# Second mixture of a four-layer chain: the shared units first, routing beside the products, normalising inside the opening

## The reference

```python
x = x + jnp.tanh(g_ffn[1]) * _L1_ffn_ref(_layernorm(x, axis=-1), ...)

shared = jax.nn.silu(h @ sWg) * (h @ sWu) @ sWd          # 256 -> 2 x 128 -> 256
routing_weights = jax.nn.sigmoid(h @ gate_w.T)           # 16 experts
topk_w, topk_idx = jax.lax.top_k(routing_weights, 8)
topk_w = topk_w / (sum(topk_w) + 1e-06) * 2.5
comb = zeros((T, 16)).at[arange(T)[:, None], topk_idx].add(topk_w)
g, u = h @ Wg[e], h @ Wu[e]                              # for every e: 256 -> 128
eo = silu(g) * u @ Wd[e]                                 # 128 -> 256
result = shared + einsum('eth,te->th', eo, comb)
```

## Time and profile before

| | |
|---|---|
| median of 3 runs | 2523.2 us (2521.43 to 2532.25) |
| profiled execution | 2521.86 us, span 2520.1 us |
| mean granted clock of TensorE | 0.935 |
| busy over the span: PE, PEld | 2187.3 us (87%), 1830.6 us (73%) |
| DVE, ACT, POOL | 1848.3 us (73%), 1290.9 us (51%), 1241.4 us (49%) |
| second mixture: rstd ready to last addition | 1322.0 to 1679.95 us of the span |

### The profile page before, as it was taken

How to read it: one execution, slowest core, us unless ns; L and a number is a source line. 1 busy time by engine, 2 the same in 40 slices (tenths; PEclk the granted TensorE clock), 3 DMA queues, 4 the chain that set the end, 5 groups by cost and what they waited for, 6 DMA issues and landing times. The chain is left out here.

```text
span 2520.1 us, 44844 instructions
## 1 busy us (share of the span) xinstructions
PE 2187.3 (87%) x15434; PEld 1830.6 (73%) x15434; DVE 1848.3 (73%) x3715; ACT 1290.9 (51%) x3127; POOL 1241.4 (49%) x1693
## 2 busy tenths in 40 slices
PE   5969997599999889999976999978999993649996
PEld 2358886488888778888866888867888871327775
DVE  5856665699999899999974777764555547966775
ACT  2113332788888877888843333322444442436763
POOL 4903442699999889999960111102344431221112
PEclk9979998799999999999996999988999995769998
DMA  4201111200000110000003000010000000010001
GB/s 133 71 34 67 68 67 38 86 18 16 18 16 14 55 47 16 18 16 20 5 27 95 26 20 26 20 51 12 8 8 8 5 1 0 1 46 23 23 19 35
DMA packets 38639, 80.39 MB, mean 32 GB/s; under 512 B 5904, under 2 KB 25680, under 8 KB 34384
## 3 DMA queue, kind: packets, MB, share of 16 engines
q1 hardware_dynamic: 38416, 77.52, 9.2%
HBM read 64.92 MB, written 12.58 MB: 31 GB/s over the span
## 5 line engine op out<-in xcount | busy, mean ns | idle before, releaser
L1229 PE MATMUL bank<-l_wr,l_xq 128*128 128x256 f32 (+1 forms) x1024 | 214.9, 353 | 7.4 <-ACT l_raw L1338 7.4
L793 PE MATMUL bank<-m_xr,m_wgr 128*128 128x512 f32 x864 | 210.8, 393 | 9.2 <-POOL m_wgr L853 9.2
L793 PEld LDWEIGHTS bank<-m_xr,m_wgr 128*128 128x128 f32 x864 | 158.8, 190 | 39.4 <-issue 9.2
L1564 POOL TENSOR_TENSOR l_tiny<-l_tiny,l_minus_half 128x6 f32<-128x6 f32 x128 | 175.8, 1373 | 10.7
L1229 PEld LDWEIGHTS bank<-l_wr,l_xq 128*128 128x128 f32 x1024 | 160.0, 194 | 25.2 <-issue 8.3
L1266 PE MATMUL bank<-l_wpr,l_cat 128*128 128x256 f32 x1024 | 167.5, 306 | 1.9 <-POOL l_cat L1615 1.9
L1908 POOL TENSOR_TENSOR l_pr<-l_pr,l_rowsum 128x512 f32<-128x512 f32 x64 | 66.5, 1040 | 205.6 <-DVE l_rowsum L1875 205.6
L853 POOL TENSOR_TENSOR m_wgr<-m_wg,m_wgr 128x512 fp32r<-128x512 f32 x18 | 23.2, 1291 | 286.7 <-ACT m_wgr L831 286.7
L1352 ACT ACTIVATE xn_T<-bank,l_head_b,l_head_w 128x512 f32<-128x512 f32 x128 | 99.6, 778 | 117.5 <-PE bank L1277 117.5
L1496 DVE TENSOR_TENSOR l_raw<-l_raw,l_tiny 128x768 f32<-128x768 f32 x128 | 158.6, 1239 | 0.0
L1244 PE MATMUL bank<-xn_T 128*128 128x128 f32 x1024 | 140.0, 280 | 17.5 <-ACT xn_T L1324 15.9
(11 more groups left out here) (316 smaller groups left out, 6280.1 us busy)
## 6 DMA issues: line engine op xcount, KB each, us to landing
l_stage<-in_l_w SPq DMA_DIRECT2D x8, 1024.0 KB, 4.7
l_centred<-l_stage SPq DMA_DIRECT2D x6, 1024.0 KB, 4.1
l_stage<-l_centred SPq DMA_DIRECT2D x6, 1024.0 KB, 4.8
m_unsplit<-in_m_w SPq DMA_DIRECT2D x14, 384.0 KB, 3.2
m_wg<-in_m_gu SPq DMA_DIRECT2D x18, 256.0 KB, 2.6
x_norm<-in_ctxT_b SPq DMA_DIRECT2D x32, 128.0 KB, 2.0
l_stage<-in_l_wp SPq DMA_DIRECT2D x4, 1024.0 KB, 4.9
l_saved<-l_xs SPq DMA_DIRECT2D x16, 256.0 KB, 2.0
```

The costliest lines, as they stand in the source:

```text
L793: r = e.matmul(banks[2 * (q % 2) + half][0:M, :], WGR[:, u % 2, a, k, sub, half, :], XR[:, b, k, cols], start=k == 0 and n == 0, stop=k == ...
L1229: r = e.matmul(to, XQ[:, q % 2, v, k, :], WR[:, j, part, k, h0 * P:h1 * P], start=k == 0 and part == 0, stop=k == KT - 1 and part == 1)
L1564: pool_own.did(e.tensor_tensor(r0, var, minus_half[:, :], ALU.pow))
```

## The change

`moe` becomes `moe1`, for this mixture alone.

- The shared units come first (steps 0 to 7), with the plain gate as share; the routed units follow. The shares `CG` are wanted from step 8 on (`add` waits for the routing there).
- SP loads units 0 and 1 and the router first, then the 13 tensors of the later attention, then the other units. ScalarE raises unit 0 during the layer norm's statistics.
- VectorE normalises groups 0 to 11 (four more buffers), GpSimd first lowers unit 0's weights and then normalises groups 12 to 15. TensorE turns groups in fours, two groups a bank; ScalarE makes two copies of each bank (`XT` and the high part). The third and fourth quarter are turned behind the first and second gate/up block.
- The router, padded to 32 columns, is now the stationary operand, and four groups go to four quarters of a bank's partitions (32 each). The products stand in two halves between the gate/up blocks; the logits are copied, turned back, and copied again. The sigmoid comes behind step 4's put, the maxima behind the additions of VectorE's step 5, the matches in steps 6 and 7, the rest in step 8.
- Per step VectorE adds the result of step n - 2 instead of n - 1.
- Weights are raised behind the put of a unit's third step instead of its second.
- The last four additions are each followed by four `bn_stats`, and the later attention's layer norm no longer counts.

```diff
-                e.wait_ge(*route(1))
-                e.wait_ge(*xlo(8))
-                for t in range(2, N + 3):
...
+                turn(e, 0)
+                turn(e, 1)
+                up_project(e, 0)
+                turn(e, 2)
+                up_project(e, 1)
+                route_matmul(e, 0, banks[6])
+                e.wait_ge(*logits_in(1))
+                turn(e, 3)
+                down_project(e, 0)
+                up_project(e, 2)
+                e.wait_ge(*xhi(8))
+                route_matmul(e, 1, banks[6])
+                up_project(e, 3)
+                turn_logits(e)
+                down_project(e, 1)
+                down_project(e, 2)
+                for n in range(4, N + 1):
+                    if n < N:
+                        up_project(e, n)
+                    down_project(e, n - 1)
...
+                put_x(e, 0)
+                put_x(e, 1)
+                for n in range(N):
+                    u = n // 4 + 1
+                    gate(e, n)
+                    if n == 0:
+                        put_x(e, 2)
+                    if n == 1:
+                        put_x(e, 3)
+                    if n == 2:
+                        keep_logits(e, 1, banks[6])
+                    if n == 3:
+                        keep_turned(e)
+                    put_high(e, n)
+                    if n == 0:
+                        keep_logits(e, 0, banks[6])
+                    if n % 4 == 2 and u < UNITS:
+                        raise_gu(e, u)
+                        raise_down(e, u)
+                    if n == 4:
+                        e.wait_ge(*lturn_in(1))
+                        e.activation(pr[:, :, :], lg[:, :, :, 0:E].rearrange("p g m w -> p (g m) w"),
+                                     ACT.Sigmoid).then_inc(prob.sem, 1)
...
             def gpsimd(e):
                 begin(e, ends)
+                lower_gu(e, 0)
+                lower_down(e, 0)
+                e.wait_ge(*norm(12))
+                for b in range(12, B):
+                    normalise(e, b)
+                for u in range(1, UNITS):
+                    lower_gu(e, u)
+                    lower_down(e, u)
...
             def vector(e):
                 begin(e, ends)
+                for b in range(12):
+                    normalise(e, b)
+                lower_x(e, 0)
+                lower_x(e, 1)
+                for n in range(N + 2):
+                    if 1 <= n <= N:
+                        lowest(e, n - 1)
+                    if n < N:
+                        hide(e, n)
+                    if n in (0, 1):
+                        lower_x(e, n + 2)
+                    if n >= 2:
+                        add(e, n - 2)
+                        if n - 2 >= N - 4:
+                            count(e, n - 2)
+                    if n == 5:
+                        route_top(e)
+                    if n in (6, 7):
+                        route_mark(e, n - 6)
+                    if n == 8:
+                        route_share(e)
...
+                    for k in range(KT):
+                        for m in range(4):
+                            b = 4 * g + m
+                            r = e.matmul(bank[W * m:W * (m + 1), g * P:(g + 1) * P], router[:, k, :], XT[:, k, b * P:(b + 1) * P],
+                                         start=k == 0, stop=k == KT - 1)
...
-            prepared_ends = layernorm(ends, counted=False) + [loaded(n_loaded)]
+            prepared_ends = layernorm(ends) + [loaded(n_loaded)]
```

More of the change, by code:

```diff
@@ L732, in moe @@
             TERMS = ((0, 0), (0, 1), (1, 0))
-            shared = units - E
-            N, Q = 4 * units, 4 * units * subs
+            xn = sb(scratch, "m1_xn", [P, 4, D])
+            l1_ends = ends
             rin = signals("router_loaded", 1, 16)
[L737 to L740, removed]
+            wg_in = Slots(signals, "weights_loaded", UNITS, 16, 2)
@@ L744, in moe @@
[L744 to L753, removed]
+            up = signals("up_projected", N)
@@ L754, in moe @@
+            silu = signals("silu", N)
+            hid = signals("hidden", N)
+            high = signals("moe_high", N)
+            low = signals("moe_low", N)
             down = signals("down_projected", N)
             acc = signals("moe_added", N)
[L757 to L769, removed]
+            bn = signals("x_counted", B)
@@ new lines, in gate, with put_high, keep_logits @@
+            def gate(e, n):
+                e.wait_ge(*up(n + 1))
+                if n >= 2:
+                    e.wait_ge(*hid(n - 1))
+                e.activation(SG[:, n % 2, :], banks[2 * (n % 2)][:, :], ACT.Silu).then_inc(silu.sem, 1)
+            def put_high(e, n):
+                e.wait_ge(*hid(n + 1))
+                if n >= 2:
+                    e.wait_ge(*down(n - 1))
+                e.copy(HBR[:, n % 2, 0, :], HT[:, n % 2, :]).then_inc(high.sem, 1)
+            def keep_logits(e, i, bank):
+                e.wait_ge(*logits(i + 1))
+                e.copy(lt[:, 2 * i:2 * i + 2, :].rearrange("p g t -> p (g t)"), bank[:, 2 * i * P:(2 * i + 2) * P]).then_inc(logits_in.sem, 1)
@@ L875, in routing, with count, route_top @@
+            def count(e, n):
+                e.wait_ge(*acc(n + 1))
+                for b in range(4 * (n % 4), 4 * (n % 4) + 4):
+                    e.bn_stats(stats[:, b, :], X[:, b, :]).then_inc(bn.sem, 1)
+            def route_top(e):
+                e.wait_ge(*prob(1))
                 for b in range(B):
@@ L945, in moe @@
-            stage(sync=sync, tensor=tensor, scalar=scalar, vector=vector, gpsimd=gpsimd)
-            return [acc(N), down(N), high(Q), wds(units)]
+                for b in range(12):
[9 more added lines that the diff above has]
+                        lower_x(e, n + 2)
+                    if n >= 2:
+                        add(e, n - 2)
[7 more added lines that the diff above has]
+                        route_share(e)
@@ L948, in l1_staging @@
+            stage(tensor=tensor, scalar=scalar, vector=vector, gpsimd=gpsimd)
+            return [bn(B), acc(N), down(N), high(N), wds(UNITS)]
         def l1_staging(scope):
```

363 lines of the change are left out of this document (192 added, 171 removed).

## The result

The changed kernel takes 2495.45 us (median of 4, 2494.7 to 2496.72) against 2523.38 for the kernel before (median of 4, the three runs shown and one more). The ratio is 0.9876, 95% interval 0.9863 to 0.9889. The profiled execution took 2496.72 (span 2494.9, mean granted clock 0.94): 25.1 less than the profiled one of before. The whole times are only good to a few us: the two medians as they stand differ by 27.9, the ratio makes it 31, and over all 31 runs of the kernel before that are on record it took from 2520.94 to 2533.64. The mechanism is therefore read from the length of the stage.

The account below looks back on a forecast made before the run. TensorE was taken to set the steady pace, after an opening of 40.0 us without large products. Opening 22.4, routing -3.9 and tail 2.2 sum to 20.7 us gained: 2502 us, range 2494 to 2511.

Parts of the forecast that it names:

- I charge both to VectorE, 2.0: Opening: GpSimd's first two weight subtractions, starting with VectorE's normalisations, delay VectorE by 2.0 us; bounds 0 and 2.0.
- the 1.3 for GpSimd's normalisation: Opening: one GpSimd normalisation falling between VectorE's two subtractions for x's low part costs 1.3 us; bounds 0 and 2.6.
- the 0.39 a group: Opening: VectorE normalises twelve groups at 0.39 us each, 4.7 us in all.
- so the first took 4.4: Opening: the first gate/up block runs mostly at half clock and takes 4.4 us; bounds 2.75 and 5.5.
- I take 2.4: Opening: each half of the four-strip router products takes 2.4 us; bounds 0.9 and 3.5.
- Routing, -3.9: Steps 5 to 8: routing beside the products stalls TensorE by 1.8, 0.1, 0.6 and 1.4, losing 3.9 us; bounds 0 and 9.2.
- The raise, 0: Each unit's weight raise, one step later, still meets VectorE's subtraction and gains 0 us; bounds -0.58 and +1.2 a unit.
- The 0.58: Extra us of a weight-raising step, 4.76 against 4.18, read as GpSimd's subtraction lengthening VectorE's; taken as unchanged over 16 units.
- the raise no longer collides: Rival, each unit's raising step: VectorE or GpSimd shifts and the collision goes, 9.3 us more gain, 2493; chance 0.07.
- The tail, 2.2: Stage end: statistics in fours behind the last additions gain 2.2 us; last down block kept at 2.77.
- The loads at nothing: SP's queue: the 13 later-attention loads, wanted 360 us later, cost nothing in their new place behind unit 0's transfers.
- The first gate/up block starts near 1331: Opening, sign to look for: first gate/up block near 1331, sixth near 1361; wrong if the first is later than 1336.

Follow-up runs that it names:

- the two runs with the loads ahead: Changed kernel with the 13 later-attention loads and router ahead of units 0 and 1: 2515.36 us; the same with unit 0's raise behind x's first copies: 2511.94 us.
- The run with the late first block: Changed kernel with the first gate/up block made to wait for GpSimd's last normalisation: 2502.91 us in one execution.
- the two runs at 0.9849 and 0.9844: Against the changed kernel: GpSimd's wait with the raise back at the second step, 0.9849; GpSimd's wait with routing's last piece split over steps 8 and 9, 0.9844.

## Why the prediction was right and wrong

The sign, the place and the order of the parts were right; the opening was priced too high, and the steps that failed are three of its terms. The stage is 7.5 us shorter than forecast, and 6.7 of them are there. Against the forecast's offsets from the first normalisation:

| milestone | forecast | measured |
|---|---|---|
| first gate/up block starts | 9.2 | 6.7 |
| it ends | 13.6 | 9.5 |
| second block through, router begins | 17.2 | 13.2 |
| fourth block through | 30.2 | 23.9 |
| down blocks behind the logits' turn | 31.5 | 25.3 |
| sixth block starts | 39.1 | 32.4 |

- **"I charge both to VectorE, 2.0" and the 1.3 for GpSimd's normalisation: failed, together with the 0.39 a group 2.5 us.** GpSimd's two subtractions lengthened VectorE's first four normalisations from 1.38 to 2.73, so 1.35 were charged by the trace (1.38 for four also in the two runs with the loads ahead, where GpSimd comes later). A group without GpSimd beside it took 0.32 (four in 1.38, the next four starting 1.30 later) and not the 0.39 of the old row, 0.8 less over twelve. GpSimd's normalisation held up nothing: VectorE's first two subtractions for x took 1.28, 0.64 each, as in the run in which GpSimd stood idle beside them (1.29 for two). It was GpSimd that paid: its four normalisations took 6.16, and 4.85 in the run in which VectorE was idle. Single ones (GpSimd's timeline):

```profile
1329.54 2.19 POOL L961 TENSOR_SCALAR m_xn<-x_resident,ln_mean,ln_rstd 128x256 f32<-128x256 f32 x1 [3.17 <-DVE x_norm L961]
...
1333.28 1.22 POOL L961 TENSOR_SCALAR m_xn<-x_resident,ln_mean,ln_rstd 128x256 f32<-128x256 f32 x1
```

The two beside VectorE's subtractions took 2.19 and 1.56, the two behind them 1.22 each, as alone. The Trainium skill's GPSIMD Engine Reference (Specifications) names VectorE instructions with two SBUF inputs as contenders for the shared interface. Here such instructions met GpSimd twice: at the raise VectorE lost 0.93 (1.61 against 0.68), in the opening GpSimd lost 1.3 over two. The traces agree with the page that the two contend.
- **"so the first took 4.4": failed, 1.55 us.** I took a block at half clock from a row that stood behind a long stretch at 0.50 and 9.16 us of idle time, and named 2.75, the case in which the transposes "leave it high", as the bound. The bound was the truth, 2.85. The run with the late first block gives 4.55: the row was right for a kernel in which TensorE had been idle for long, and my own chain, with 1.39 us between transposes and block, did not have that.
- **"I take 2.4" for a router half: failed, 2 x 1.3 us.** A half took 1.08, and the time from the end of the third block to the fourth's start (1341.29 + 2.75 to 1345.14) is 1.1, all told. The lower bound of 0.9, scaled from the two-strip row, was near; the middle that I took was no row's. The Trainium skill's TensorEngine Tiling (Array Packing), section Key Properties, has the different tiles of the array work in parallel, and by it I had written about 1 us each and a gain of 25. The trace agrees: eight transposes at full clock, full width and also 128 columns moving, take 1.04 (the next block starts 0.79 behind their start), which makes an estimated 3.2 to 4.2 for 32, and the strips take 1.08 for 32. The run with the wide router, 3.65, prices the old form, in which other operands move. The hand-offs of 0.5 were about as charged.
- **Routing, -3.9: right, 3.45 lost.** The stalls came as 1.46, 0.1 (in the records 1369.46 begins 0.1 late), 0.35 and 1.21, against 1.8, 0.1, 0.6 and 1.4.
- **The raise, 0: right.** 17.31 a unit; undoing the move costs 1.0 in one place only. The 0.58 itself I took as given. The rival "the raise no longer collides", 9.3 us, did not occur, but the run with one wait shows its price right: 9.1.
- **The tail, 2.2: near by its sum (2.6), half by its reason.** The statistics bring 1.3; the rest is the clock in the last down block, which I had kept at 2.77.
- **The loads at nothing: right for the new order, and the cover was named (360 us).** I did not price the other side, and the old order in the new kernel would cost 20 us.
- **"The first gate/up block starts near 1331": met by luck.** It started at 1330.78, but only because the first normalisation stood 2.1 us later than before; from there it was 6.7 us and not 9.2.

All three errors of the opening lay on one side, since I went for the upper or middle price in each place that no row showed. The range allowed 5 us downward for the opening, although the lower bounds written beside its terms add up to 8.0 below the middle (2.0, 1.3, 1.65 and twice 1.5).

The best version run is the changed kernel with the one wait of GpSimd: 2485.9 us, 0.9841 of before; the two runs at 0.9849 and 0.9844 have the same wait and can't be told from it.

## What to carry to other kernels

Price a block's clock by a row in which TensorE did ahead of it what it will do in your own chain, idle time and narrow products both, not by the row of the same name. Where several unknown prices are bounded, write down whether you lean the same way in each: three leanings of 1.5 to 2.6 us made 6.7 of the 7.5 us by which the stage was missed. And where two engines meet in SBUF at a fixed place in each round, try first to order them by a wait: here one line brought 9.1 us, a third of what the whole rearrangement did.

## What the runs showed of the hardware that was not expected

- GpSimd's and VectorE's holding-off has no fixed loser; in both places the one that began second was the longer. At the raise GpSimd began at 1438.90 and VectorE at 1439.14, and VectorE's subtraction took 1.61 instead of 0.68. In the opening VectorE began at 1329.35 and GpSimd at 1329.54; VectorE's two took 1.28, unharmed, and GpSimd's normalisation 2.19 instead of 1.22.
- SP's own issue of a transfer took 3.63 and 4.22 us when 15 and 16 transfers had been issued just ahead, and 3.27 and 2.80 in the other run with the loads ahead, where most take 0.3 to 0.8. So a row of transfers can hold up the engine that issues, not only the data; why at these two was not tested.
- Idle time is not all that takes the clock away. With the wide router TensorE was busy without a gap and the next block still ran at 0.50 (4.28 against 2.91).
- A stall of 1.84 us ahead of a down block was followed by a gate/up block of 4.42 us, while stalls of 1.46 were not; a stall of 2.15 at the end of the stage was followed by a down block of 1.69, stalls of 2.35 and 2.51 by 2.77 and 2.45. What decides there stays open.
